# A graph attention kernel: TensorE's semaphores raised from a drain behind each set of matmuls, or from the set's last matmul

## What is computed

```python
h = relu(layernorm(x))                      # 12500 x 128
h = (h @ W_node.T).reshape(nodes, 4, 32)
e = (edge_attr @ W_edge.T).reshape(edges, 4, 32)
att = sum(concat([h[src], h[tgt], e], -1) * a, -1)        # edges x 4
att = where(att > 0, att, 0.2 * att)
m = maximum(segment_max(att, tgt), 0.0)
ex = exp(att - m[tgt])
denom = segment_sum(ex, tgt) + (num_edges - deg)[:, None] * exp(-m)
w = ex / denom[tgt]
out = x + segment_sum(w[:, :, None] * h[src], tgt)
```

## Time and profile before

| | us |
|---|---|
| median of three timed runs | 2500.19 |
| lowest and highest | 2499.8, 2505.36 |
| span of the profiled execution | 3117.4 |
| first score reduction (L1125) of the loop, in the profiled execution | 180.4 |
| last one | 3053.4 |

### The profile page before, as it was taken

How to read it: one execution, slowest core, us unless ns; L and a number is a source line. 1 busy time by engine, 2 the same in 40 slices (tenths; PEclk the granted TensorE clock), 3 DMA queues, 4 the chain that set the end, 5 groups by cost and what they waited for, 6 DMA issues and landing times. The chain is left out here.

```text
span 3117.4 us, 35586 instructions
## 1 busy us (share of the span) xinstructions
PE 1323.3 (42%) x8927; PEld 1088.2 (35%) x8928; DVE 1439.7 (46%) x3481; ACT 613.5 (20%) x1206; POOL 1527.1 (49%) x1632
## 2 busy tenths in 40 slices
PE   6353345334444344543443444334353434344343
PEld 5132334333433333432333333333333333333333
DVE  8324345335444353543444445435453345354447
ACT  5121122112112121111121121112121112112112
POOL 5545545545554545455455355464454544544430
PEclk9666676666667676666676677667676666666666
DMA  6443433333434334343343243333333333323224
GB/s 194 114 124 91 112 84 95 106 84 93 115 85 112 92 93 116 80 113 90 80 113 89 78 112 96 94 101 83 99 103 97 87 92 81 87 74 77 72 68 154
DMA packets 324638, 306.36 MB, mean 98 GB/s; under 512 B 55245, under 2 KB 287597, under 8 KB 318167
## 3 DMA queue, kind: packets, MB, share of 16 engines
q1 hardware_dynamic: 273255, 196.39, 20.4%
q0 software_dynamic: 50304, 107.57, 15.6%
q10 hardware_dynamic: 880, 0.13, 0.0%
HBM read 175.10 MB, written 18.15 MB: 62 GB/s over the span
## 5 line engine op out<-in xcount | busy, mean ns | idle before, releaser
L154 POOL DMA_INDIRECT gath<-node_table,src_i x1563 | 1481.7, 948 | 1463.2 <-DMA gath<-gath 699.9
L1262 DVE TENSOR_TENSOR acc<-acc,bank 128x411 f32 x622 | 333.3, 536 | 1410.8 <-remote 655.6
L959 PEld LDWEIGHTS bank<-vals,onehot 128*128 128x128 f32 x3288 | 709.6, 281 | 20.9
L959 PE MATMUL bank<-vals,onehot 128*128 128x137 f32 x3288 | 700.7, 372 | 0.0
L956 PE MATMUL bank<-block_1h,zero_b 128*128 128x411 bf16 x519 | 249.1, 480 | 795.1 <-issue 293.4
L1033 ACT COPY onehot_t<-ps_oht 128x2048 bf16<-128x2048 bf16 x104 | 194.1, 1866 | 1156.9 <-remote 686.9
L1042 ACT CAST onehot<-onehot_b 128x384 f32<-128x384 bf16 x622 | 269.2, 475 | 488.2 <-remote 279.9
L956 PEld LDWEIGHTS bank<-block_1h,zero_b 128*128 128x128 bf16 x519 | 64.9, 125 | 823.0 <-issue 329.9
L921 PE MATMUL ps_oht<-ident_b,onehot_b 128*128 128x128 bf16 x1664 | 155.5, 268 | 411.8 <-DVE onehot_b L1109 298.6
L921 PEld LDWEIGHTS ps_oht<-ident_b,onehot_b 128*128 128x128 bf16 x1664 | 138.2, 123 | 418.6 <-DVE onehot_b L1109 301.5
L1223 DVE TENSOR_TENSOR vals<-gath,bank 128x2048 f32<-128x2048 f32 (+1 forms) x103 | 234.3, 2275 | 9.2 <-ACT bank L1046 9.1
(11 more groups left out here) (215 smaller groups left out, 1095.1 us busy)
## 6 DMA issues: line engine op xcount, KB each, us to landing
gath<-gath SPq DMA_DIRECT2D x1664, 66.0 KB
eattr<-edge_attr_in SPq DMA_DIRECT2D x46, 1024.0 KB
gath<-node_table,src_i POOLq DMA_INDIRECT x1563
node_table<-onehot_b SPq DMA_DIRECT2D x14, 462.0 KB, 4.1
gath<-x_in SPq DMA_DIRECT2D x14, 448.0 KB, 4.8
edge_scores<-edge_out SPq DMA_DIRECT2D x49, 64.0 KB
gath<-edge_attr_in SPq DMA_DIRECT2D x3, 1024.0 KB
edge_s<-edge_scores SPq DMA_DIRECT2D x12, 256.0 KB
```

The lines of the kernel that those rows point to most:

```text
L154: nc.gpsimd.indirect_dma_start(out=ring[:, t % RING, :], out_offset=None, in_=table, in_offset=bass.IndirectOffsetOnAxis(ap=src_i[:, t:t + ...
L959: last = T.matmul(at, onehot[:, b % 3, j % 3, :], weighted(g, a)[:, j, :], start=not wide, stop=j == BATCHES[b][-1])
L1262: V.tensor_tensor(a_blk, a_blk, SUM_BANK[b % 3][:, 0:wide * ACC], ALU.add).then_inc(s["added"], 1)
```

## The change

On TensorE, in the loop over groups, the increment is taken off the last matmul of each set and put on a drain that is issued behind the set. A drain is an instruction of the sequencer that waits until the engine is empty. Which semaphores are raised, how often and in which order, stays as it was, and so do all other engines' queues. `target_parts` has a drain in its second half only. The last set of transposes at the loop's start (`tgt_ps`) and the front stage keep their form.

```diff
                         for c in range(3 * HEADS):
-                            last = T.matmul(ps_tgt_slot[:, c * G:(c + 1) * G], tgt_t[0:N_BLOCKS, c, :],
+                            T.matmul(ps_tgt_slot[:, c * G:(c + 1) * G], tgt_t[0:N_BLOCKS, c, :],
                                             block_1h[0:N_BLOCKS, ds(g.n * G, G)], start=True, stop=True)
-                        last.then_inc(s["tgt_slot_ps"], 1)
+                        T.drain().then_inc(s["tgt_slot_ps"], 1)
...
-                        last.then_inc(s["edge_ps"], 1)
+                        T.drain().then_inc(s["edge_ps"], 1)
...
-                        last.then_inc(s["edge_turned"], 1)
+                        T.drain().then_inc(s["edge_turned"], 1)
...
-                        last.then_inc(s["oht_ps"], 1)
+                        T.drain().then_inc(s["oht_ps"], 1)
...
                         if a == 1:
-                            last.then_inc(s["scores_ps"], 1)
+                            T.drain().then_inc(s["scores_ps"], 1)
 
                     def spread_drop(g):
                         pe.wait_ge(s["drop_diag"], g.n + 1)
-                        T.matmul(ps_drop, ones[:, :], drop_diag[:, :], start=True, stop=True).then_inc(s["drop_ps"], 1)
+                        T.matmul(ps_drop, ones[:, :], drop_diag[:, :], start=True, stop=True)
+                        T.drain().then_inc(s["drop_ps"], 1)
...
                             for j in BATCHES[b]:
                                 at = into[:, ds(places[g.n, a][j], ACC)] if j % SPAN else into[:, 0:ACC]
-                                last = T.matmul(at, onehot[:, b % 3, j % 3, :], weighted(g, a)[:, j, :], start=not wide, stop=j == BATCHES[b][-1])
-                            last.then_inc(s["sum_ps"], 1)
+                                T.matmul(at, onehot[:, b % 3, j % 3, :], weighted(g, a)[:, j, :], start=not wide, stop=j == BATCHES[b][-1])
+                            T.drain().then_inc(s["sum_ps"], 1)
```

More of the change, by code:

```diff
@@ L902, in edge_scores @@
                         for c in range(4):
-                            last = T.matmul(ps_edge, w_eatt[:, c, :], eattr_of(t)[:, c, :], start=(c == 0), stop=(c == 3))
-                        last.then_inc(s["edge_ps"], 1)
+                            T.matmul(ps_edge, w_eatt[:, c, :], eattr_of(t)[:, c, :], start=(c == 0), stop=(c == 3))
+                        T.drain().then_inc(s["edge_ps"], 1)
                     def turn_edges(c, targets_copied):
@@ L912, in turn_edges @@
                             for k in range(max(c - 1, 0), c + 1):
-                                last = T.matmul(ps_turned[:, h, :], edge_s[:, k % 2, h, :], sel_f[:, k - c + 1, :], start=(k == max(c - 1, 0)), stop=(k == c))
-                        last.then_inc(s["edge_turned"], 1)
+                                T.matmul(ps_turned[:, h, :], edge_s[:, k % 2, h, :], sel_f[:, k - c + 1, :], start=(k == max(c - 1, 0)), stop=(k == c))
+                        T.drain().then_inc(s["edge_turned"], 1)
                     def onehot_transposes(g, a):
@@ L920, in onehot_transposes @@
                         for j in range(GS):
-                            last = T.transpose(ps_oht[:, j, :], onehot_b[:, g.r, a * GS + j, :], ident_b[:, :])
-                        last.then_inc(s["oht_ps"], 1)
+                            T.transpose(ps_oht[:, j, :], onehot_b[:, g.r, a * GS + j, :], ident_b[:, :])
+                        T.drain().then_inc(s["oht_ps"], 1)
                     def target_parts(g, a):
@@ L933, in target_parts @@
                             slot = a * GS + j
-                            last = T.matmul(ps_te[:, 3 * HEADS * slot:3 * HEADS * (slot + 1)], onehot_t[:, j, :], tgt_slot[:, :, slot],
+                            T.matmul(ps_te[:, 3 * HEADS * slot:3 * HEADS * (slot + 1)], onehot_t[:, j, :], tgt_slot[:, :, slot],
                                             start=True, stop=True)
                         if a == 1:
-                            last.then_inc(s["scores_ps"], 1)
+                            T.drain().then_inc(s["scores_ps"], 1)
                     def spread_drop(g):
                         pe.wait_ge(s["drop_diag"], g.n + 1)
-                        T.matmul(ps_drop, ones[:, :], drop_diag[:, :], start=True, stop=True).then_inc(s["drop_ps"], 1)
+                        T.matmul(ps_drop, ones[:, :], drop_diag[:, :], start=True, stop=True)
+                        T.drain().then_inc(s["drop_ps"], 1)
                     def sums(g, a, batches):
```

## The result

The changed kernel takes 2504.05 us (median of 14 runs, 2498.76 to 2513.13), the kernel before 2499.79 us beside it (14 runs, 2492.63 to 2505.36). The medians are 4.3 us apart. The ratio is 1.0025 with an interval of 1.0014 to 1.0036, which is 3.5 to 9 us: a small slowdown, within the 0.3% that the prediction took as no change. The forecast was 2540 us and "slower". The rival "Covered" is what happened.

What follows compares the result with a forecast made beforehand. GpSimd's gathers were taken as the bound, 44.1 us per turn. Compute loop 37.1 + 7.3 = 44.4, plus 0.5 for coupling, 44.9; 180.4 + 51 x 44.9 + 64 + 6 = 2540 us, range 2508 to 2650 (8 in 10: 2485 to 2680).

Steps and rivals of the forecast that it cites:

- Covered: Rival: the compute loop, at 42.3 us with c nearer 0.3, stays under GpSimd's pace; 2500 us, chance 0.39.
- the whole cover of 7 us is used up: Per group, drains lengthen the compute loop from 37.1 to 44.4 us, level with GpSimd's 44.1.
- the 0.5 us of coupling: Per turn, two level chains coupled by waits take 0.5 us more than either, making 44.9 us.
- 180.4 before the first turn: Time before the loop's first turn, 180.4 us from the profiled execution, subtracted from the timed median to get the turn.
- The drains' sum: All on-path TensorE drains and exposed register loads: 7.3 us per group, 14 c + 1.0, from 4.5 to 12.2.
- c: Cost of one TensorE drain on the path: 0.45 us, with 0.25 and 0.8 as the ends.
- The batches' drains: Drains behind TensorE's batches of sums, each costing c on the path, with 0.45 us deducted for cover in the first half.
- the 1.3 us of the register loads: Second half of a turn: two TensorE register loads, formerly beside the transposes, start only after them, adding 1.3 us.
- Dear restart: Rival: a drain costs 0.8 us by restarting from empty or waiting out late increments; 49.3 us per turn, 2765 us, chance 0.11.
- Faster: Rival: the drain's increment passes late matmul increments that hold the compute loop; 2454 to 2492 us, chance 0.08.
- No effect at all: Rival: a drain raises its semaphore before TensorE's matmuls have ended; no time or chance given.
- The closing remark: If the compute loop already bounds the timed run, the 7.3 us count in full: 372 us, 2872 us in all.

Runs made afterwards that it cites:

- the long condition: Stretch of executions in which TensorE's completions come late; the unchanged kernel before took 3113.22 us there (median of 17 runs).
- before, second execution: The kernel before, unchanged, profiled once more: one run, 2495.31 us, span 2492.7 us.
- k2_sums: Kernel before with GpSimd waiting for the gather block two back, and drains behind the batches of sums alone: 2181.66 us, ratio 0.8733.
- k2_others: Changed kernel with GpSimd waiting for the gather block two back, without the drains behind the batches of sums: 2193.61 us, ratio 0.8791.
- k2_hoist: Changed kernel with GpSimd waiting two blocks back and the first half's register loads issued ahead of the transposes' wait: 2211.09 us, ratio 0.8855.
- all_but_tail2: Kernel before with drains everywhere but in the last two groups and what follows, run again: 2494.08 us, ratio 0.9993.
- tail_only2: Kernel before with drains in the last two groups and what follows alone, run again: 2504.44 us, ratio 1.0033.
- after_again: The changed kernel, unchanged, run again in the long condition: 3544.32 us, ratio 1.14 to the kernel before.
- k2_before: Kernel before with GpSimd waiting for the landing of the gather block two back, not the last one: 2140.09 us, ratio 0.8557.
- k2_before2: Kernel before with GpSimd waiting for the gather block two back, run again in a later session: 2140.46 us, ratio 0.8576.

## Why the prediction was wrong

**What bounds the kernel: right.** GpSimd sets the timed run with a turn of 44.9 us, inside the 43.2 to 45.6 us worked out from the earlier trace rows, and the compute loop of 37.1 us was 36.7. The copies' wait that the earlier trace rows show was rightly put down to the compute loop.

**The step that failed: "the whole cover of 7 us is used up".** The prediction set a loop of 37.1 + 7.3 = 44.4 us against GpSimd's 44.1, and took both as level. Measured were 42.4 us against 44.9: the loop stayed under GpSimd's pace. Two terms were mis-sized, the cover by 1.1 us and the drains by 1.7, and a third, the 0.5 us of coupling, hangs on the two.

**The cover: 7.0 us, measured 8.1.** It was too small because of "180.4 before the first turn". That was taken from the earlier trace rows, an execution in the long condition, and carried over to timed runs that lack it; before, second execution, has 137.5. The prediction had noted that its profile "is not like the timed ones", worked the turn out anew from the median, and left the start uncorrected. The 64 us behind the last turn were 66.3, and the 6 around the span were 2.6. With 137.5 in place of 180.4 the same sum gives (2500.2 - 137.5 - 64 - 6) / 51 = 44.95, and the turn was 44.88 and not 44.1.

**The drains' sum: 7.3 us per group, measured 5.6** (5.8 where nothing covers them). Three terms of it:
- c, 0.45 us, was 0.38 at half clock and 0.40 at full. With the lost overlap (0.21 or 0.16) and 0.05 for the drain as reckoned, 0.12 to 0.19 are left for the restart, not 0.2.
- The batches' drains, 10 c less 0.45 of cover and with 0.1 at the ends, would be 3.6 us at c = 0.39; k2_sums measured 2.0. More of them was covered than I had seen. In the timeline after, the batch at 1556.44 still waits 1.00 us for ScalarE's cast, where it waited 0.94 before: its cover isn't used up. Which other drains among these are covered wasn't taken apart.
- The others, four c, the 1.3 us of the register loads and 0.05, would be 2.9 us at c = 0.39; k2_others measured 2.7. The register loads are where the prediction put them: the gap of 1.53 us in the kernel after, 0.23 in k2_hoist.

Missing from the sum was the clock. The passes' mean rose from 363 to 384 ns, so (384 - 363) / 155 = 0.14 of them fell to half clock: 0.14 x 63 x 0.11 = 0.9 us per turn, an estimate (by a count of the passes over 400 ns it is 0.53 and 0.64, and 0.8 us). So the drains with what they expose are some 4.7 us of the 5.6, where the sum had 7.3.

**The coupling of two level chains: 0.5 us, measured nothing** (all_but_tail2, 0.9993), because there were no two level chains here. The size was not the mistake: k2_sums, whose chains are nearly level, shows 0.44 us. Of the forecast's 40 us, 25.5 were this coupling (51 x 0.5) and 15.3 a loop 0.3 us over GpSimd (51 x 0.3). Both rest on a cover of 7.0 and a cost of 7.3, a comparison of two terms each known to about 1 us. That the predicted turn of 44.9 us is so near the measured ones (44.88 before, 45.10 after) is luck: it was reached by adding 0.8 us for the drains to a turn of 44.1 that was 0.8 too low. The stated range did hold the time.

**What was missing: the uncovered end.** The text multiplied by 51 turns and looked for no cost where gathers are over. There the cover is nil, and by tail_only2 and all_but_tail2 the few us that the change costs come from there.

**The rivals.** "Covered" asked for a loop of 42.3 us, and it was 42.4. The mechanism is the one that it names, but its number agrees partly by luck: it has c at 0.3 us, and c was 0.39, with fewer of the drains on the path. "Dear restart" fell in these timed runs: behind batches c stayed under 0.45. Its second half, that "a drain makes TensorE wait them out", is what the long condition shows, with 49.3 us per turn said and 64.5 there, where a turn without drains has 56.3. "Faster", by drains that pass the late increments, fell: after_again's drains end late with the completions. The Trainium skill's "Perfetto Trace Analysis", section "Per-engine timelines", says that an update goes out only when PSUM has acknowledged the writes, and that TensorE's end times are modelled. A drain of 14.3 us behind transposes of 1.89 us is in keeping with it, but no row shows that the acknowledgement is what was late. "No effect at all" fell too: the median drain ends 0.02 us behind the last matmul. The closing remark, 372 us if the compute loop bounds the run already, is near the 431 us of the long condition, but not for its reason alone: the drains cost 8.45 us per turn there and 5.6 elsewhere, against 7.3 said.

**What would show it.** (1) A batch's drain costs 0.38 or 0.40 us, 0.4 to 0.5 was said: at its lower edge. (2) The drains end 0.02 us behind the matmuls, 0.05 was said: right in kind. (3) The register loads' place: right. (4) A turn 7 us longer: 5.6. (5) More idle time for copies out of the ring: no, 46.2 and 49.7 us, as it must be where the cover holds.

## What to carry to other kernels

Ask what a change costs the loop that it stands in, and apart from that what covers this loop: here 5.6 us per turn disappeared under a wait of 8.1 us, and the same 5.6 us became 213 us in the kernel that waits one block further back. Before a difference of 1 us is relied on, every part of the sum (the start and the end as well as the turn) has to come from an execution like the timed ones, and the stretch where the cover ends is priced by itself. On TensorE a drain is over 0.02 us behind the last matmul here; what it costs is the overlap that it takes away. Of the 5.6 us per turn, 1.3 were register loads of the sequencer that had run beside matmuls, an estimated 0.9 passes that fell to half clock, and the rest the restarts of the stream.

## What the runs showed of the hardware

- A drain behind a batch of matmuls cost 0.38 us at half and 0.40 us at full clock, one between slots 0.54 us at half clock (means over the two of a batch). Raising the semaphore from it or from the matmul made no difference (2504.05 and 2504.02 us, loops of 42.37 and 42.33).
- In a whole stretch of runs TensorE's completions came late, as the drains' ends show (up to 14.3 us for a drain): the kernel before took 3113 us there (median of 17 runs, 3088 to 3125) and 2495 to 2500 us beside all other experiments, with the same program. One chip showed both, at different times. The mean granted clock was lower with it (0.627 in after_again, 0.715 in the kernel after), but the clock doesn't account for the time: the passes' mean is 398 ns against 384, an estimated 0.6 us per turn of the 19.4 by which it is longer. What brings this about is open; no run was made for its cause, and a profile with a span far from its median should be read as evidence on its own condition only.
- A gap of 1.3 us on TensorE was taken out once per turn, and an estimated 1.25 us came back beside it through the clock: in the second to the fifth batch behind it more of the passes ran at full clock, the passes' mean over the whole kernel fell from 371 to 343 ns, the mean granted clock rose from 0.742 to 0.795.
- GpSimd's wait for the landing of the previous eight gathers cost 380 us in 174 waits (2.2 us each). Waiting for the block before that one instead took 359 and 355 us off the kernel (k2_before, k2_before2), and the gathers themselves were no slower (951 ns each against 950).
